# Node chain of a graph layer: its intermediate in a PSUM bank, the bias added by VectorE, and another order of the first loads

## The chip, the cores and the metric

One core of a Trainium2 chip runs the whole kernel in one launch. The metric is the time on the device in microseconds; of several runs the median counts. The engines have names of their own in the profile: PE is TensorE (PEld its weight loads), DVE is VectorE, ACT is ScalarE, POOL is GpSimd, SP is SyncE, which here only starts transfers.

## What is computed

Two layers with residuals, on x of 6250 rows by 512 and a graph of 106250 edges sorted by target:

```python
x = x + gnn(layernorm(x))       # h = x @ W_self + b_self + mean_over_edges(x[src]) @ W_neigh
                                # layernorm(h) * gamma + beta; h < 0 times alpha; plus x
x = x + ffn(layernorm(x))       # 16 experts, top 2 by a gate; h = silu(x @ w1.T) is averaged
                                # over the tokens of an expert, y = mean @ w2.T,
                                # out = sum over the two picks of softmax weight * y[expert]
```

Everything is float32. The kernel gets that from pairs of float16 numbers, a high and a low part, and three matmuls in place of one (high x high, high x low, low x high).

## The kernel before

A tile is 128 rows of x; there are 49 (TILES), the last with 106 rows. The engines run programs of their own, and semaphores alone order them; each program is written out in the order of work.

**Table (0 to 204 us).** For each tile: SP loads x into one of 8 buffers; VectorE takes the statistics (`stats_of`, L1225) and aggregates; `scales_of` turns four tiles' variances into scale and offset, for the first two groups of four on VectorE (L1236 to L1246), from the third on POOL (L579 to L599). ScalarE applies them (`normal`, L665), TensorE transposes (`turn_x`, L907), ScalarE takes the high part (L673), VectorE the low (`turned_low`, L1251), TensorE multiplies by W_neigh in 12 matmuls (`project`, L861), ScalarE and VectorE take both parts of the result (L681, L1257), and SP stores it to a table in DRAM. Before the first projection VectorE finds the largest weight of W_neigh (L1290), a power of two is derived from it, ScalarE writes the high part of the weights in one instruction (L684) and VectorE the low in one (L1300). ScalarE's queue starts the loads of all weights (L652, L657); SP's queue starts the edge lists (L381 to L389) and then x. Between tiles VectorE has other lists (`lists`): the edge bookkeeping behind tiles 1 to 15, and `self_maxima`, `self_bias`, `self_low` behind tiles 17, 23 and 25. In `self_bias` six instructions write b_self as a high row and a low row of `bparts`.

**Steps (204 to about 1310 us).** 106250 edges are 208 groups of 512; a group can span tiles, so there are 257 steps. POOL fetches 128 rows of 2 KB of the table per indirect gather, four gathers per group (L617), into a ring of four groups; in front of a group it waits for the step that freed the slot. In `step` TensorE adds the rows into the bank of the target tile with one-hot matrices (L960) and counts (L963). Banks 0 and 1 alternate by tile. In the first 45 steps TensorE also computes a `side` per step: bias by one matmul of `kilo` and `bparts` (L934), then x @ W_self in 12 matmuls, in banks 5 and 6, which ScalarE brings to `slots`.

**Node chain.** When a tile's edges are all in, VectorE runs `gnn` (L1324 on): count, sum times share plus self term into `slots` (L1344), memset of the banks (which frees them for the tile after next, `c_ev`), moments, gamma and beta (L1356, L1357), the slope (L1358, L1359), the residual with x loaded anew (L1362), moments, and high and low part of the normalized row (L1367 to L1369). The intermediates `hb`, `ub`, `x2f` lie in SBUF. In tiles 0 to 15 it also takes the maximum of an expert's w1 (L1372), in tiles 20 to 35 it splits w1 in two parts (L1379, L1382), which SP stores and later loads back.

**Tail of the steps.** In the last 49 steps TensorE turns finished tiles (`turn_x2`, L976, through bank 4) and computes gate logits (`gate`); ScalarE copies the turned tile (`take_turned`, L729). VectorE routes the first 32 tiles (`route(0)`) between tiles 46 and 47 and reads their positions, which `place(0)` leaves in bank 5, in `rows_to(0)` between tiles 47 and 48. Then come `route(1)`, the maps, and the first expert gather (L633).

**Experts and output (1373 to 1685 us).** 48 slots of tokens through the experts on TensorE, then the output.

## Time and profile before

| | |
|---|---|
| median of 3 runs | 1687.58 us (1685.50 to 1687.65) |
| profiled execution | 1686.77 us |
| its span, first to last instruction | 1685.0 us |
| busy: PE, DVE, ACT, POOL | 1217.9, 1028.5, 886.9, 992.6 us |
| mean granted TensorE clock | 0.887 of full speed |
| DMA, mean over the span | 228 GB/s |

The profile is of one execution. The busy times are sums over stages with different limits, so none of them is near the span; what matters in a stage is which wait ends last there. Times of matmuls are modelled, and their pitch (start to start) is more telling than their length.

### The profile page before, as it was taken

The numbers are of one execution on the slowest core, as the hardware profiler recorded it, in microseconds if no ns is written. First come the engines' busy times: TensorE is split into PE (matmuls) and PEld (weight loads), VectorE is DVE, ScalarE is ACT, GpSimd is POOL, SyncE is SP. The second block draws the span as 40 slices with busy tenths as digits, with TensorE's granted clock in tenths as the row PEclk, the third lists the DMA queues.
The fourth block names the chain that finished last, engine by engine and source line by source line (L and its number), as shares of the span: only waits on it lengthen the run. The fifth ranks groups of instructions, "written<-read, shape, count | busy, mean of one in ns | idle before, by whom it ended". The sixth has DMA issues, their size and how long they took to land.

```text
span 1685.0 us, 37100 instructions
## 1 busy us (share of the span) xinstructions
PE 1217.9 (72%) x7688; PEld 644.5 (38%) x7696; DVE 1028.5 (61%) x2918; ACT 886.9 (53%) x1932; POOL 992.6 (59%) x1193
## 2 busy tenths in 40 slices
PE   4989899999665555665565546666677159999876
PEld 2545444444322222222222222234444146777612
DVE  6676235546666665657566655655658966666626
ACT  3455445555644444444444444446667838888402
POOL 2223277676777777777777777777776025555200
PEclk9999999999988888778878897799999669999885
DMA  5445277777888887888888888778877526666547
GB/s 194 141 139 166 108 219 252 243 250 225 265 265 268 264 245 237 280 260 296 261 281 279 285 279 275 240 237 249 246 233 219 216 80 201 199 200 205 192 167 275
DMA packets 141638, 384.99 MB, mean 228 GB/s; under 512 B 22911, under 2 KB 23041, under 8 KB 141509
## 3 DMA queue, kind: packets, MB, share of 16 engines
q0 software_dynamic: 75840, 248.18, 48.9%
q1 hardware_dynamic: 62392, 130.43, 21.8%
q10 hardware_dynamic: 3276, 4.97, 0.9%
q8 instruction: 43, 0.70, 0.2%
q14 instruction: 87, 0.70, 0.1%
HBM read 323.78 MB, written 59.72 MB: 228 GB/s over the span
## 4 chain that ended last, share of the span: by engine, by line
PE 39%; POOL 24%; issue 16%; DVE 9%; DMA 7%; POOLq 2%; SPq 2%; ACT 1%; DVEq 0%; ACTq 0%
POOL work L617 24%; PE ps L861 13%; PE ps L960 10%; PE ps L1053 6%; DMA work<-table,work 4%; PE ps L1064 3%; PE ps L1055 3%; POOLq L612 2%; PE ps L1113 1%; SPq L525 1%; DMA work<-in_w_t 1%; DMA work<-in_x 1%; PE ps L907 1%; DVE slots L1515 1%; PE ps L934 1%
## 5 line engine op out<-in xcount | busy, mean ns | idle before, releaser
L617 POOL DMA_INDIRECT work<-table,work x832 | 828.4, 996 | 295.6 <-issue 239.8
L960 PE MATMUL ps<-work 128*128 x2056 | 574.6, 431 | 345.0 <-DMA work<-table,work 329.5
L960 PEld LDWEIGHTS ps<-work 128*128 128x128 f16 x2056 | 216.4, 106 | 589.9 <-issue 445.3
L715 ACT ACTIVATE work<-work,ones 128x512 f16<-128x512 f16 x259 | 185.3, 715 | 325.7 <-PE ps L963 325.2
L709 ACT ACTIVATE work<-iota_row,work 128x128 f16<-128x128 f32 x1040 | 331.3, 390 | 31.6 <-ACT work L715 23.9
L861 PE MATMUL ps<-wparts,slots 128*128 128x512 f16 x1176 | 274.1, 383 | 12.2 <-DVE slots L1251 12.2
L1339 DVE TENSOR_SCALAR inv<-ps 128x1 f32 (+2 forms) x49 | 7.7, 158 | 336.6 <-PE ps L963 331.9
L633 POOL DMA_INDIRECT slots<-x_d,betab x114 | 107.8, 946 | 161.8 <-PE ps L1064 83.9
L861 PEld LDWEIGHTS ps<-wparts,slots 128*128 128x128 f16 x1176 | 115.8, 99 | 139.8 <-DVE slots L1251 14.7
L1053 PE MATMUL ps<-work,wparts 128*128 x456 | 156.1, 382 | 2.2 <-ACT wparts L801 2.0
L801 ACT COPY wparts<-ps 128x1024 f16<-128x1024 f16 x114 | 115.3, 1012 | 59.8 <-PE ps L1064 59.1
L1055 PE MATMUL ps<-work,wparts 128*128 x456 | 125.0, 274 | 0.0
L1553 DVE TENSOR_REDUCE work<-ps 128x256 f32<-128x512 f32 x114 | 78.7, 691 | 41.4 <-PE ps L1055 40.3
L963 PEld LDWEIGHTS ps<-onesh,work 128*128 128x128 f16 x1028 | 68.3, 102 | 76.5 <-issue 28.5
L729 ACT COPY wparts<-ps 128x1024 f16<-128x1024 f16 (+1 forms) x49 | 49.4, 1009 | 81.3 <-PE ps L976 80.2
L721 ACT ACTIVATE slots<-ps,wscale 128x512 f32<-128x512 f32 (+1 forms) x49 | 33.6, 686 | 103.0 <-PE ps L861 103.0
L1545 DVE TENSOR_TENSOR slots<-slots,work 128x256 f32 x114 | 52.8, 464 | 39.2 <-issue 24.5
L1064 PE MATMUL ps<-identh,slots 128*128 128x128 f16 x912 | 70.8, 221 | 5.1 <-DMA slots<-x_d,betab 5.1
L1064 PEld LDWEIGHTS ps<-identh,slots 128*128 128x128 f16 x912 | 61.4, 99 | 20.3 <-issue 5.3
L681 ACT ACTIVATE work<-ps 128x512 f16<-128x512 f32 (+1 forms) x49 | 29.2, 596 | 75.7 <-PE ps L861 75.7
L587 POOL TENSOR_SCALAR var<-mv 128x4 f32<-128x4 f32 x11 | 2.5, 228 | 108.3 <-DVE mv L1233 108.3
L963 PE MATMUL ps<-onesh,work 128*128 128x1 f16 x1028 | 64.1, 166 | 0.0
(283 smaller groups left out, 1577.5 us busy)
## 6 DMA issues: line engine op xcount, KB each, us to landing
work<-in_x SPq DMA_DIRECT2D x96, 256.0 KB, 2.8
work<-in_w_t SPq DMA_DIRECT2D x48, 512.0 KB, 7.6
work<-table,work POOLq DMA_INDIRECT x832
table<-work SPq DMA_DIRECT2D x48, 256.0 KB, 2.0
x_d<-work SPq DMA_DIRECT2D x48, 256.0 KB
x_d<-slots SPq DMA_DIRECT2D x48, 256.0 KB
out_x<-slots SPq DMA_DIRECT2D x48, 256.0 KB
slots<-x_d SPq DMA_DIRECT2D x41, 256.0 KB
```

Source lines behind the costliest of these rows:

```text
L617: pool.indirect_dma_start(out=gath[:, g % GRING, w, :], out_offset=None, in_=table[:, :], in_offset=bass.IndirectOffsetOnAxis(ap=idx_all[: ...
L633: pool.indirect_dma_start(out=xf[:, b, :], out_offset=None, in_=x2_d[:, :], in_offset=bass.IndirectOffsetOnAxis(ap=idx2[:, k:k + 1], axis= ...
L709: last = act.activation(away[:, par, w, :], iota_row[:, :], ACT.Abs, bias=negd[:, ds(GT * k + w, 1)])
L715: act.activation(hot[:, slot, :, :], away[:, slot % 2, :, :], ACT.Relu, bias=ones[:, 0:1], scale=-1.0).then_inc(c_hot, 1)
L801: act.copy(xft[:, b, :, :, :], chunks16(bank16(6 + n % 2), P)).then_inc(f_xt, 1)
L861: last = pe.matmul(to, left(a, c), right(w, c), start=start and c == 0 and a == 0 and w == 0, stop=c == n - 1 and a == 1)
L960: pe.matmul(ps[:, ds(bank, 1), :], hot[:, s, w, :], gath_row[:, ds(at + (2 * w + half) * D, D)].unsqueeze(1), start=False, stop=True, skip ...
L963: last = pe.matmul(ps[:, BANKS:2 * BANKS, 0:1][:, ds(bank, 1), 0], hot[:, s, w, :], onesh[:, :], start=False, stop=True, skip_group_check= ...
L1053: pe.matmul(ps[:, HBANK + b, :].rearrange("p (u a n) -> p u a n", u=1, a=2), xft[:, b, 0, c, :], both, start=c == 0, stop=c == CHUNKS - 1, ...
L1055: last = pe.matmul(ps[:, HBANK + b, FF:2 * FF].unsqueeze(1), xft[:, b, 1, c, :], high, start=False, stop=c == CHUNKS - 1, skip_group_check ...
L1064: last = pe.transpose(bank16(6 + n % 2)[:, j * P:(j + 1) * P], xf[:, b, j * P:(j + 1) * P], identh[:, :])
L1553: dve.tensor_reduce(hid[:, b, :], ps[:, HBANK + b, :].rearrange("p (a n) -> p n a", a=2), X, ALU.add).then_inc(f_pre, 1)
```

## The change

- `gnn`: PSUM bank 4 (`draft`) is the intermediate. L1344 writes there, a tensor_tensor adds `bself` on VectorE, and each instruction that had `hb`, `ub` or `x2f` beside another SBUF tensor has one input from the bank. `hb` stays in SBUF for one of them. `ub` and `x2f` are gone.
- `side`: the bias matmul is gone, and so are `kilo`, `bparts` and their preparation. `bself` stays in SBUF until the last tile, so expert 14's part of w1, which lies over it, is among the last four loaded.
- w1 split: the low part is written in two halves, each by a tensor_scalar into the bank and a tensor_tensor from it.
- `turn_x2` goes through bank 5, with new waits in front of it and of `place(0)`.
- Start: SP loads x 0 to 3 ahead of the edges; the other weights are loaded from POOL's queue behind its `scales_of(0)`; all scales are now POOL's; the W_neigh parts are written in four chunks each, behind `normal(0)` and `normal(1)`, and TensorE waits for them chunk by chunk.

```diff
@@ block.sync
+            for i in range(HALF):
+                load_x(i)
             early = (GROUP_CHUNKS - 1) * P * GE_EDGES
...
-            for i in range(UNROLL):
+            for i in range(HALF, UNROLL):
                 load_x(i)
...
-            for e in list(range(9)) + list(range(12, EXPERTS)):
+            for e in list(range(9)) + [12, 13, 15]:
                 load_w1s(e)
...
-            for e in range(9, 12):
+            for e in (9, 10, 11, 14):
                 load_w1s(e)
@@ block.gpsimd
-            for q in range(2, PARTS):
+            scales_of(0)
+
+            for to, what in ((ws[:, :, :], w_self.rearrange("(c p) n -> p c n", p=P)),
+                             (gw[:, :, :], gate_t.rearrange("(c p) n -> p c n", p=P)),
+                             (bself[:, :], b_self.to_broadcast([P, D])), (alphab[:, :], alpha.to_broadcast([P, 1])),
+                             (gammab[:, :], gamma.to_broadcast([P, D])), (betab[:, :], beta.to_broadcast([P, D]))):
+                pool.dma_start(to, what).then_inc(s_w, 16)
+
+            pool.wait_ge(s_const, 2)
+            for n, s in enumerate(c_g):
+                pool.dma_start(spare[16 * n:16 * (n + 1), :],
+                               zero[16 * n:16 * (n + 1), :].bitcast(f16)).then_inc(s, 16 * GT)
+            pool.dma_start(x2_d[0:1, :], zero[0:1, :].bitcast(f16)).then_inc(d_zero, 16)
+
+            for q in range(1, PARTS):
                 scales_of(q)
@@ block.scalar
-            act.wait_ge(w_scale, 1)
-            act.activation(wnp[:, 0, :, :], wn[:, :, :], ACT.Copy, scale=wscale[:, 0:1]).then_inc(w_hi, 1)
             normal(0)
             normal(1)
+            act.wait_ge(w_scale, 1)
+            for c in range(CHUNKS):
+                act.activation(wnp[:, 0, c, :], wn[:, c, :], ACT.Copy, scale=wscale[:, 0:1]).then_inc(w_hi, 1)
@@ block.tensor
-                pe.matmul(to, kilo[:, 0:rows], bparts[:, :], start=True, stop=False)
-                split_mm(to, lambda a, c: xt[:, i, a, c, 0:rows], lambda w, c: wsp[:, w, c, :], CHUNKS,
-                         start=False).then_inc(c_mm, 1)
+                split_mm(to, lambda a, c: xt[:, i, a, c, 0:rows], lambda w, c: wsp[:, w, c, :], CHUNKS).then_inc(c_mm, 1)
...
-                if i:
-                    pe.wait_ge(d_xt, i)
+                pe.wait_ge(d_xt, i) if i else pe.wait_ge(c_self, 2 + TILES)
+                if i == TILES - 2:
+                    pe.wait_ge(i_row, 1)
...
                     if late and k == STEPS - 2:
+                        pe.wait_ge(d_xt, k - LATE)
                         place(0)
@@ block.vector, gnn
+                u, u1 = draft[r, :], draft[r, :].unsqueeze(1)
...
-                ln.link(dve.scalar_tensor_tensor(slot, ps[r, bank, :].unsqueeze(1), share, slot, ALU.mult, ALU.add))
+                ln.link(dve.scalar_tensor_tensor(u1, ps[r, bank, :].unsqueeze(1), share, slot, ALU.mult, ALU.add))
...
+                ln.link(dve.tensor_tensor(u, u, bself[r, :], ALU.add))
...
-                ln.link(dve.scalar_tensor_tensor(hb[r, :].unsqueeze(1), slot, mean, gammab[r, :].unsqueeze(1), ALU.subtract, ALU.mult))
-                ln.link(dve.scalar_tensor_tensor(hb[r, :], hb[r, :], guess[r, 0:1], betab[r, :], ALU.mult, ALU.add))
-                ln.link(dve.tensor_scalar(ub[r, :], hb[r, :], 0.0, alpha_less[r, :], ALU.min, ALU.mult))
-                ln.link(dve.scalar_tensor_tensor(ub[r, :], ub[r, :], shift1, hb[r, :], ALU.add, ALU.add))
+                ln.link(dve.scalar_tensor_tensor(u, u, mean, gammab[r, :], ALU.subtract, ALU.mult))
+                ln.link(dve.scalar_tensor_tensor(hb[r, :], u, guess[r, 0:1], betab[r, :], ALU.mult, ALU.add))
+                ln.link(dve.tensor_scalar(u, hb[r, :], 0.0, alpha_less[r, :], ALU.min, ALU.mult))
+                ln.link(dve.scalar_tensor_tensor(u, u, shift1, hb[r, :], ALU.add, ALU.add))
...
-                dve.scalar_tensor_tensor(x1, x1, up1, ub[r, :], ALU.mult, ALU.add).then_inc(d_x1, 1)
+                dve.scalar_tensor_tensor(x1, x1, up1, u, ALU.mult, ALU.add).then_inc(d_x1, 1)
...
-                dve.tensor_scalar(x2f[r, :], x1, mean, unit, ALU.subtract, ALU.mult)
+                dve.tensor_scalar(u, x1, mean, unit, ALU.subtract, ALU.mult)
                 ln.link(dve.tensor_scalar(hi, x1.unsqueeze(1), mean, unit, ALU.subtract, ALU.mult))
-                dve.tensor_tensor(lo, x2f[r, :].unsqueeze(1), hi, ALU.subtract).then_inc(d_x2, 1)
+                dve.tensor_tensor(lo, u1, hi, ALU.subtract).then_inc(d_x2, 1)
...
-                    dve.scalar_tensor_tensor(halved[:, :, 1, :], stage[:, :, :], wscale[:, 3:4], halved[:, :, 0, :],
-                                             ALU.mult, ALU.subtract).then_inc(v_split, 1)
+                    for h in range(2):
+                        cs = slice(h * CHUNKS // 2, (h + 1) * CHUNKS // 2)
+                        u2 = draft.rearrange("p (c n) -> p c n", c=CHUNKS // 2)
+                        dve.tensor_scalar(u2, stage[:, cs, :], wscale[:, 3:4], None, ALU.mult).then_inc(v_hi, 1)
+                        dve.wait_ge(v_hi, 4 * (j - SPLIT_AT) + 2 + 2 * h)
+                        dve.nop(nofuse=True)
+                        lo2 = dve.tensor_tensor(halved[:, cs, 1, :], u2, halved[:, cs, 0, :], ALU.subtract)
...
```

## Rows read from the trace of the kernel before

**Rows 1.** The page, the chain that ended last, by line.
```profile
POOL work L617 24%; PE ps L861 13%; PE ps L960 10%; PE ps L1053 6%; DMA work<-table,work 4%; PE ps L1064 3%; PE ps L1055 3%; POOLq L612 2%; PE ps L1113 1%; SPq L525 1%; DMA work<-in_w_t 1%; DMA work<-in_x 1%; PE ps L907 1%; DVE slots L1515 1%; PE ps L934 1%
```

**Rows 2.** The gathers' line L617: durations, then what POOL sat idle for (us, times).
```profile
L617 POOL DMA_INDIRECT work<-table,work x832: 940/946/1771, 204.0 to 1299.1; - x167
  issue: 239.8, 787
  PE ps L963: 28.1, 44
```

**Rows 3.** Chain of waits, 1255 to 1385 us: start, us, what.
```profile
1266.87 0.76 DVE slots L1344
...
1372.87 0.94 POOL slots L633
```

**Rows 4.** Groups by line, POOL, 424 to 1263 us: busy, mean ns | idle.
```profile
L617 POOL DMA_INDIRECT work<-table,work x644 | 643.8, 1000 | 196.2 <-issue 186.8 <-PE ps L963 9.4
```

**Rows 5.** Timeline, a split tile, 716 to 720 us: start, us, engine, line.
```profile
716.48 0.55 DVE L1367 TENSOR_SCALAR work<-work,norm 128x512 f32<-128x512 f32 x1
716.54 1.06 POOL L617 DMA_INDIRECT work<-table,work  x1 [0.30 <-issue]
...
719.10 1.28 DVE L1382 SCALAR_TENSOR_TENSOR work<-work,wscale 128x1024 f16<-128x1024 f32 x1
...
719.44 1.76 POOL L617 DMA_INDIRECT work<-table,work  x1 [0.30 <-issue]
```

**Rows 6.** Windows: us; busy PE, PEld, DVE, ACT, POOL; clock, DMA share, GB/s.
```profile
686.00:1032.00 346.00, 198.49 (x961) 91.44 (x962) 225.03 (x698) 158.97 (x400) 266.73 (x261) 0.83 0.86 278
```

**Rows 7.** Chain of waits, 217 to 227 us, a pattern of 45 pitches.
```profile
217.57 0.24 PE ps L934
217.80 2.59 PE ps L861 x12
...
222.20 0.24 PE ps L934
```

**Rows 8.** Groups by line and form, DVE, 686 to 1032 us.
```profile
L1382 DVE SCALAR_TENSOR_TENSOR work<-work,wscale 128x1024 f16<-128x1024 f32 x15 | 19.3, 1284 | 1.8
...
L1369 DVE TENSOR_TENSOR slots<-work,slots 128x512 f32 x15 | 10.4, 692 | 2.2
...
L1367 DVE TENSOR_SCALAR work<-work,norm 128x512 f32<-128x512 f32 x15 | 8.3, 554 | 0.6
...
L1358 DVE TENSOR_SCALAR work<-work,alpha_less 128x512 f32<-128x512 f32 x16 | 7.8, 487 | 0.6
L1346 DVE MEMSET ps<- 128x512 f32 x15 | 7.3, 485 | 0.9
...
L1339 DVE TENSOR_SCALAR inv<-ps 128x1 f32 x15 | 2.4, 157 | 82.0 <-PE ps L963 78.2 <-issue 3.9
```

**Rows 9.** Timeline of the start.
```profile
7.82 2.29 DVE L1290 TENSOR_REDUCE wmax<-work 128x1 f32<-128x2048 f32 x1 [7.68 <-DMA work<-in_w_neigh]
...
16.82 0.38 DVE L1238 BATCH_NORM_AGGREGATE mv<-stats 128x2 f32<-128x6 f32 x4
...
19.96 0.16 DVE L1246 TENSOR_SCALAR gb<-nmr 128x4 f32<-128x4 f32 x1
...
23.54 3.33 PE L861 MATMUL ps<-wparts,slots 128*128 128x512 f16 x12
...
34.24 4.45 PE L861 MATMUL ps<-wparts,slots 128*128 128x512 f16 x12 [3.90 <-DVE slots L1251]
```

**Rows 10.** Timeline of POOL, 36 to 45 us: first and last of a scale chain.
```profile
38.34 0.25 POOL L587 TENSOR_SCALAR var<-mv 128x4 f32<-128x4 f32 x1 [27.97 <-DVE mv L1233]
...
43.38 0.22 POOL L599 TENSOR_SCALAR gb<-nmr 128x4 f32<-128x4 f32 x1
```

**Rows 11.** Chain of waits, 84 to 130 us, around the bias list.
```profile
104.28 2.78 PE ps L861 x12
...
111.73 2.76 PE ps L861 x12
```

More of the change, by code:

```diff
@@ L236, in build @@
         wall = cut(P)
-        assert place[0] <= WORK - TABLES
+        assert place[0] <= BSELF_AT
         BT = BATCH[0][1]
@@ L554, in _ @@
             pool.memset(onesh[:, :], 1.0)
-            pool.memset(kilo[:, :], SCALE)
             pool.memset(zero[:, :], 0.0)
@@ L1288, in _ @@
             dve.wait_ge(s_const, 1)
+            for i in part_tiles(0):
+                last = stats_of(i)
+            ln.link(last)
+            dve.nop(nofuse=True)
+            scales_of(0)
             dve.wait_ge(s_wn, 16)
```

110 lines of the change are left out of this document (43 added, 67 removed).

## The prediction

> **What bounds the kernel now.** I read the page's chain first: one line, L617, the indirect gathers of the step stage, carries 24% of the span as POOL work [rows 1]. The line's own view says how such a gather goes: typically 946 ns, at worst 1771, and in front of 787 of 832 of them POOL waits for nothing that shows, 239.8 us in all, 0.305 each [rows 2]. So a bare gather costs 0.946 + 0.305 = 1.251 us. The same view puts TensorE in front of 44 gathers, 28.1 us; less the 0.305 that every gap has, 28.1 - 44 x 0.305 = 14.7 us are real waits, for steps that free a ring slot. After 424 us no gap is longer than the usual one, so all 14.7 lie before it.
>
> From that I see four stretches. From 0 to 204 us the table is built: TensorE, now and then held up by VectorE. From 204 to about 424 TensorE is the bound, which there has the self terms beside the steps. From 424 to 1264 it is POOL, gather behind gather. From 1267 it is VectorE: tile 46, the first routing batch, tiles 47 and 48, routing and maps, to the first expert gather at 1372.87 [rows 3]. Behind that the change touches nothing that is late.
>
> The gathers of the third stretch aren't bare: 644 of them take 643.8 us where 644 x 0.946 = 609.2 would do, 34.6 too much [rows 4]; in the 346 us with the w1 split 261 take 266.7 in place of 246.9, 19.8 too much [rows 6]. The timeline shows who lengthens them [rows 5]: the gather that starts 0.34 us into the 1.28 us scalar_tensor_tensor of the w1 split (L1382, two SBUF inputs) takes 1.76 us and ends 0.82 behind that instruction's end. One that starts with a tensor_scalar (L1367, one SBUF input) takes 1.06.
>
> **The change, part by part.**
>
> *The intermediate in PSUM.* The large instructions of a node chain with two SBUF inputs are L1356, L1357, L1359, L1362, L1369, and L1382 in 16 tiles. Each of them gets one input from bank 4 instead, or (L1382) gives way to tensor_scalars into the bank and tensor_tensors out of it. If two SBUF inputs are what holds a gather, the 34.6 us go, but for what L1368 and L1379 do, which keep one SBUF input and an SBUF output. A hit costs 1.06 - 0.95 = 0.11 us by the row [rows 5]; one hit in each of some 40 tiles would be 4.4, I take a third, 1.6 (bounds 0 and 8, the latter in the first rival): -33.0 us. POOL waits for nothing else here, so this is the span's, as long as the transfers follow: the DMA engines are busy 0.86 [rows 6], and the same bytes in 4% less time are 0.90.
>
> The Trainium skill (SBUF — State Buffer, Who interferes with whom) says that a VectorE instruction with two SBUF inputs contends with a GpSimd instruction that reads SBUF and that the later one is blocked; the gather of 1.76 us agrees. It also says that a tensor_scalar in a two-port mode blocks GpSimd for its whole length; the gather of 1.06 us, which started with the 0.55 us L1367, doesn't bear that out fully. By that rule L1368 and L1379 would go on holding gathers.
>
> *The bias matmul.* In the second stretch each pitch of 4.63 us has a piece of 0.24 us of L934 on the chain [rows 7]. A matmul of 512 columns has a pitch of 2.59/12 = 0.216 there [rows 7], and 48 of the 49 lie in the stretch: -10.4 us. POOL's real waits are 14.7, which is more, so it doesn't become the bound. If some of it does, -6.
>
> *VectorE's extra work.* Per tile there is one tensor_tensor 128x512 more, 0.69 and a gap of 0.04. L1358 and L1367 have 0.49 and 0.55 us for 512 elements, where the two-input forms and L1382 (1.28 for 1024) go at half the rate; into PSUM I give them 0.75. That is +0.27 and, since L1368 starts 0.47 behind the start of L1367, +0.27. Together 1.27 us per tile [rows 8]. The one large VectorE output in PSUM that the trace has is the 0.485 us memset, so an output there costs between nothing extra and, by doubling 0.75, 0.75 more. I take nothing, as the row is near.
>
> In the middle this hides. VectorE waits 82.0 us for TensorE in front of L1339 in the 15 tiles of the split's 346 us [rows 8], 5.5 each; the tile pitch is 832/49 = 17 gathers of 266.7/261 + 0.305 = 1.33, 22.6 us. So it is occupied 17.1. To that come 1.27 and, for the split, two times 0.75, two times 0.69 and gaps of 0.3 in place of 1.28 and 0.1: +1.8. That makes 20.2 against a new pitch of 17 x 1.251 = 21.3: just hidden. In the last stretch nothing hides it: three tiles, +3.8 us.
>
> The Trainium skill (VectorE: DVE Perf Modes, The TRN2 errata) gives a PSUM source 120 fixed cycles and an SBUF source 58, 0.065 us more; by that the tail would be some 8 instructions x 3 tiles x 0.065 = 1.6 us longer. No row here shows that difference.
>
> *Turn bank and waits.* The transposes move to bank 5, where the first batch's positions come too. place(0) now waits for a ScalarE copy, with the last step behind it; VectorE comes to the positions 2.5 us later than before and to the last tile 3.8 later, so both should hide. turn_x2(47) waits until VectorE has read the positions; behind it are two gates, and on ScalarE a copy, a distance and the one-hots that SP's w1 loads wait for. The next to need any of them is tile 48's transpose, a whole node chain later. Nothing, or +3 if it doesn't hide. Four w1 loads instead of three come last; I take nothing, for the first expert gather comes some 36 us after they are issued.
>
> *Start.* Before, the first scale chain on VectorE goes from the aggregates at 16.82 to the last scale at 20.12, project(0) starts at 23.54 and project(2), behind the second such chain and the edge list, at 34.24 [rows 9]. After, x 0 to 3 come together with the neighbour weights (2 MB by about 8.5 us, an estimate from 1.5 MB by 7.8); statistics and aggregates to 9.4, POOL's scale chain of 5.3 us [rows 10] to 14.7, two normals of 0.8 to 16.2, four chunks of the high part of 0.6 to 18.6, the low part to 19.9, project(0) near 20.7: 2.9 earlier. VectorE also is rid of 2.9 of the second chain's 3.3 us: 5.8 at best by project(2), of which I take 4.5, since TensorE and ScalarE are late next. Against it: POOL issues six weight loads and five small stores ahead of scales_of(1). No row has a 512-row load in its queue. At 0.5 us each (a small one) they are hidden; at four times a gather's 0.95 for the two large ones, normal(4) comes late by 2 us. Bounds -1 and -6.
>
> *Self lists.* VectorE's bias list stops TensorE once: 7.45 us between two projections whose pitch is 3.03 each, so 1.4 are lost [rows 11]; they go, and the reduction of b_self, an instruction of 0.69, too: -2.1.
>
> **Sum:** -33.0 - 10.4 + 3.8 - 4.5 - 2.1 = -46.2 us. The span 1685.0 becomes 1638.8, and with the 1.77 that lies around it in the profiled execution (1686.77) 1640.6. The median of the runs, 1687.58, is 0.8 above that execution: 1641.4 us.
>
> **The rivals.**
> *Tensor_scalars hold gathers as well.* L1368 (0.55) and L1379 (0.75) then cover a gather's start with the chance length/1.25 and hold it for half their length: 0.12 us in each of 39 tiles and 0.22 in each of 16, 8.2 us where I have 1.6: 1648. For it speaks that L1368 would be the largest of its kind left; against it the 1.06 us. Chance 0.13.
> *The rate isn't POOL's to give.* The transfers, at 0.86 busy, can't come faster, or the two inputs aren't what lengthens a gather: only -13.2 is left, 1674. For it: 278 GB/s in the split tiles [rows 6]. Against: no wait for a slot after 424. Chance 0.10.
> *VectorE becomes the bound in the 16 split tiles.* The price is paid per output into PSUM. The two banks let it lag by one tile, 21 us, so it decides from 21.3 + 21/16 = 22.6 us a tile, and from 25.4 it eats the whole gain. At 0.75 more for each of 8 large outputs a tile takes 26.2: 16 x 4.9 - 21 = +57, and in the tail 3 x 6 x 0.75 = +13.5: 1712. Against it is the memset. Chance 0.04.
> The forecast has 0.70, with a range of its own of 1634 to 1650; 0.03 is for what I don't see.
>
> **Range and chances.** 1631 to 1661: the low end has start and self lists at their best and no residue; the high end takes the first rival, a poor start, the dearer tail and a part of the second rival. This kernel's measurement tells 0.2%, 3.4 us, from no change. The first two rivals are faster as well: faster 0.94, same 0.02, slower 0.04.
>
> **What would show it.** L617 in the third stretch at a mean of 0.95 us, none near 1.7, about 790 in all. L934 gone and the pitch 4.42 in the second. First gather at 197.4, project(0) near 20.7. L1358 and L1367 at 0.75, the wait in front of L1339 in the split tiles about 1 us each. 110 us in place of 106 from tile 46's eviction to the first expert gather. Wrong would be: gathers beside instructions with one SBUF input above 1.1 us, gathers that wait for TensorE after 415 us, large outputs in PSUM above 0.9 us, or project(2) no earlier than 33.

## The result, and the profile after

The changed kernel takes 1643.49 us (median of 4 runs, 1643.22 to 1646.05) where the kernel before takes 1686.54 (4 runs, 1684.44 to 1687.65). The ratio is 0.9746, with a 95% interval of 0.9731 to 0.9760. The profiled execution has 1643.22 us and a span of 1641.4, 43.6 less than the 1685.0 of before. Forecast were 1641.4 us.

The page's chain by line has the old order: the gathers, now line L626, still lead it, with 22% in place of 24% [rows 1], and the bias matmul's line is gone from it.
```profile
POOL work L626 22%; PE ps L866 14%; PE ps L967 11%; PE ps L1062 6%; DMA work<-table,work 5%; PE ps L1073 3%; PE ps L1064 3%; POOLq L621 2%; PE ps L1122 1%; DMA work<-in_w_t 1%; SPq L526 1%; DMA work<-in_x 1%; PE ps L912 1%; DVE slots L1520 1%; DVE slots L1486 1%
```

The gathers' own line (durations, then what POOL sat idle for, us and times). The longest gather is 1347 ns where it was 1771, the median is the same 946 [rows 2]: what a gather costs by itself has not changed, and most of the lengthened ones have gone. Of 95 gathers over 1.1 us 7 are left; the 1347 ns stand beside a two-input instruction of the routing (L1445), which the change didn't touch. The real waits for TensorE are 26.1 - 54 x 0.305 = 9.6 us; they were 14.7.
```profile
L626 POOL DMA_INDIRECT work<-table,work x832: 940/946/1347, 197.8 to 1249.8; - x167
...
  issue: 236.7, 777
...
  PE ps L970: 26.1, 54
```

Groups by line, POOL, in the stretch that it bounds, 413 to 1216 us (answers to [rows 4]): the mean is 948 ns where it was 1000. 607.9 - 641 x 0.946 = 1.5 us of excess are left of 34.6.
```profile
L626 POOL DMA_INDIRECT work<-table,work x641 | 607.9, 948 | 195.7 <-issue 184.0 <-PE ps L970 11.6
```

Windows of the same stretch and of the 326 us with the w1 split (us; busy PE, PEld, DVE, ACT, POOL; clock, DMA share, GB/s; answers to [rows 6]): the same work in less time fills the DMA engines to 0.89, at 293 GB/s, where it was 0.86 and 278. They followed.
```profile
413.00:1216.00 803.00, 487.74 (x3083) 246.65 (x3080) 590.96 (x1761) 419.34 (x1019) 607.61 (x641) 0.88 0.86 272
659.00:985.00 326.00, 190.25 (x970) 89.68 (x968) 261.67 (x736) 159.15 (x401) 246.92 (x260) 0.87 0.89 293
```

VectorE by line and form in those 326 us (answers to [rows 8]). L1379 and L1382 are the new split, L1361 and L1352 the two tensor_scalars that now write PSUM, L1362 and L1373 those that still write SBUF, L1339 the bias add. The last row is the wait for the next tile: 21.3 us for 16 of them, where it was 82.0 for 15.
```profile
L1379 DVE TENSOR_SCALAR ps<-work,wscale 128x512 f32<-128x512 f32 x30 | 22.6, 754 | 3.2
L1382 DVE TENSOR_TENSOR work<-ps,work 128x512 f16<-128x512 f32 x30 | 20.8, 692 | 3.1
...
L1361 DVE TENSOR_SCALAR ps<-work,norm 128x512 f32<-128x512 f32 x15 | 12.2, 814 | 0.6
L1336 DVE SCALAR_TENSOR_TENSOR ps<-ps,inv,slots 128x512 f32<-128x512 f32 x15 | 11.4, 759 | 3.7 <-DVE inv L1334 3.7
...
L1373 DVE TENSOR_SCALAR work<-work,wscale 128x1024 f16<-128x1024 f32 x15 | 11.3, 755 | 0.0
L1352 DVE TENSOR_SCALAR ps<-work,alpha_less 128x512 f32<-128x512 f32 x15 | 11.3, 754 | 0.5
...
L1339 DVE TENSOR_TENSOR ps<-ps,work 128x512 f32<-128x512 f32 x15 | 9.5, 636 | 0.0
L1362 DVE TENSOR_SCALAR slots<-work,norm 128x512 f32 x15 | 8.7, 581 | 0.0
...
L1331 DVE TENSOR_SCALAR inv<-ps 128x1 f32 x16 | 2.5, 158 | 21.3 <-issue 14.7 <-PE ps L970 6.7
```

The second stretch, chain of waits: a pitch is 215.24 - 210.82 = 4.42 us. The 0.24 us piece of [rows 7] is gone.
```profile
210.82 2.61 PE ps L866 x12
213.43 1.73 PE ps L967 x8
215.16 0.08 PE ps L970 x4
215.24 2.61 PE ps L866 x12
```

The end of the third stretch and of the fourth, chain of waits. Tile 46's eviction is at 1219.56 and the first expert gather at 1329.49 (1266.87 and 1372.87 in [rows 3]).
```profile
1213.78 3.10 DMA work<-table,work
...
1219.56 0.77 DVE ps L1336
...
1329.49 0.94 POOL slots L642
```

With these readings the 43.6 us of the span fall into five parts (us; start times of gathers number 0 and 160, of tile 46's eviction and of the first expert gather, and the rest):

| stretch | before | after | difference | forecast |
|---|---|---|---|---|
| start of the kernel to gather 0 | 204.0 | 197.8 | -6.2 | -6.6 |
| gather 0 to gather 160 | 220.0 | 209.9 | -10.1 | -10.4 |
| to tile 46's eviction | 842.8 | 811.9 | -31.0 | -33.0 |
| to the first expert gather | 106.0 | 109.9 | +3.9 | +3.8 |
| rest | 312.1 | 311.9 | -0.2 | 0 |

The first row isn't all the change's. In the profiled execution of before, TensorE's granted clock is 0.5 of full speed (1.2 GHz) for 3.4 us from 35.0 us on, after TensorE had been idle for 3.90 us [rows 9]; project(2) takes 4.45 us there. In that of after no such stretch comes in the table stage, TensorE had been idle for 1.78 us, and project(2) takes 2.76. So 1.7 of the 6.2 us are the clock's (windows of before and of after, columns as above).
```profile
35.00:38.40 3.40, 3.40 (x10) 1.06 (x7) 3.14 (x9) 0.00 (x0) 0.06 (x1) 0.50 0.38 132
31.20:33.90 2.70, 2.70 (x13) 1.10 (x13) 2.70 (x5) 2.20 (x4) 0.00 (x0) 1.00 0.04 14
```
It is no fixed cost of the old start: no_bias_mm below, which starts like the kernel before, takes 2.76 us there after 3.21 us of idle time, and node_only, which has the old start as well, takes 4.28 at a clock of 0.5.

### The profile page after: what moved, and what is told of

Read it like the earlier page. It is cut to its first block, busy times and chain, and to the rows that moved or that the text cites. A ratio compares the mean times of both kernels' runs of the same rounds, so it can differ in the third digit from the quotient of the medians.

```text
span 1641.4 us, 37307 instructions
## 1 busy us (share of the span) xinstructions
PE 1189.9 (72%) x7639; PEld 636.6 (39%) x7647; DVE 1109.4 (68%) x2978; ACT 887.4 (54%) x1935; POOL 966.4 (59%) x1236
## 4 chain that ended last, share of the span: by engine, by line
PE 40%; POOL 22%; issue 16%; DVE 9%; DMA 7%; POOLq 2%; SPq 1%; ACT 1%; DVEq 0%; ACTq 0%
POOL work L626 22%; PE ps L866 14%; PE ps L967 11%; PE ps L1062 6%; DMA work<-table,work 5%; PE ps L1073 3%; PE ps L1064 3%; POOLq L621 2%; PE ps L1122 1%; DMA work<-in_w_t 1%; SPq L526 1%; DMA work<-in_x 1%; PE ps L912 1%; DVE slots L1520 1%; DVE slots L1486 1%
## 5 line engine op out<-in xcount | busy, mean ns | idle before, releaser
L626 POOL DMA_INDIRECT work<-table,work x832 | 790.0, 950 | 290.6 <-issue 236.7
L967 PE MATMUL ps<-work 128*128 x2056 | 557.4, 421 | 330.6 <-DMA work<-table,work 316.4
L866 PEld LDWEIGHTS ps<-wparts,slots 128*128 128x128 f16 x1176 | 112.1, 99 | 140.0 <-DVE slots L1249 13.8
L726 ACT ACTIVATE slots<-ps,wscale 128x512 f32<-128x512 f32 (+1 forms) x49 | 33.6, 686 | 92.7 <-PE ps L866 92.7
L1255 DVE SCALAR_TENSOR_TENSOR work<-ps,work 128x512 f16<-128x512 f32 (+1 forms) x49 | 33.7, 689 | 44.1 <-ACT work L685 44.0
## 6 DMA issues: line engine op xcount, KB each, us to landing
work<-in_w_t SPq DMA_DIRECT2D x48, 512.0 KB, 12.2
```

Of the source, the lines that this page charges most:

```text
L626: pool.indirect_dma_start(out=gath[:, g % GRING, w, :], out_offset=None, in_=table[:, :], in_offset=bass.IndirectOffsetOnAxis(ap=idx_all[: ...
L866: last = pe.matmul(to, left(a, c), right(w, c), start=start and c == 0 and a == 0 and w == 0, stop=c == n - 1 and a == 1)
L967: pe.matmul(ps[:, ds(bank, 1), :], hot[:, s, w, :], gath_row[:, ds(at + (2 * w + half) * D, D)].unsqueeze(1), start=False, stop=True, skip ...
```

## Experiments: does each part bring its share alone?

All ratios are to the kernel before on the same chip, with 95% intervals. The gathers' total is the sum of the durations of the 832 gathers. Each trace is of one execution; those of no_bias_mm, node_only, dummy_ts, bias_sbuf and best are the longest of their kernel's.

**start_only.** The kernel before with the new start alone: the two loads' order, POOL's scale chains, the chunks of the neighbour weights.

> The kernel before with the new start alone (x 0 to 3 first, other weights from POOL's queue, all scales on POOL, neighbour weights in chunks); node chain, bias matmul and bias list as before. Theory: the start is worth what the table stage shows of it, 4.75 us at project(3), and the rest of the 6.2 us at the first gather comes from the shorter lists: first gather at 199.3, time 1681.8 (-4.8). Rival: the start's gain is eaten again in the table stage by VectorE's lists, so that the first gather comes less than 2 us earlier. In the gathers nothing changes: L617's total stays near 828 us.

Measured: 1687.4 us, ratio 0.9979 (0.9966 to 0.9992), -3.5 us. The first gather starts at 200.4 where it was 204.0, -3.6 and not the -4.7 expected. Project(3) starts at 35.30 where it was 40.26, 5.0 earlier, 1.7 of them by the clock as above; but then the granted clock is 0.5 for 3.4 us from 100.0 on, the projection there takes 4.45 us instead of 2.76, and 1.7 are lost again. The last gather starts at 1299.4, where it was 1299.1: the gathers' total is 833.1 us in place of 828.4, with the same longest one. So in this execution the gathers took back what the start gave, and the median shows less than was expected. What is held varies by some 4 us with nothing changed: 790.0 and 794.5 in two executions of the changed kernel (the second is after_again below).

**no_bias_mm.** The kernel before without the bias matmul; it leaves b_self out of the result.
```diff
-                pe.matmul(to, kilo[:, 0:rows], bparts[:, :], start=True, stop=False)
-                split_mm(to, ..., CHUNKS, start=False).then_inc(c_mm, 1)
+                split_mm(to, ..., CHUNKS).then_inc(c_mm, 1)
```

> The kernel before without the bias matmul (b_self is left out of the result); VectorE's preparation of it stays. Theory: TensorE is the bound while it has sides, so 48 x 0.216 = 10.4 us go, time 1676.2, and POOL's real waits for steps fall from 14.7 to about 4. Rival: POOL is as late as TensorE there, and the gathers, still lengthened, give only 6 us or less. 260 to 420 us is the only stretch that gets shorter; L617's total stays near 828.

Measured: 1680.2 us, ratio 0.9944 (0.9927 to 0.9960), -9.4 us. The gathers, source view (columns as above):
```profile
L617 POOL DMA_INDIRECT work<-table,work x832: 940/946/1770, 202.2 to 1292.9; - x167
...
  issue: 236.4, 776
...
  PE ps L961: 23.2, 55
```
The real waits are 23.2 - 55 x 0.305 = 6.4 us, 8.3 less than before. From gather 0 to gather 160 it is 210.2 us where it was 220.0, -9.8: in its stretch the matmul's 10.4 us are worth nearly all of it. The rest of this trace doesn't stand still, and its span is only 5.4 shorter: the first gather comes 1.8 earlier (the clock at project(2)), the third stretch takes 2.8 more with a total of 832.4 in place of 828.4, and from tile 46's eviction to the first expert gather it is 110.1 us in place of 106.0, since VectorE waits 4.15 us for TensorE's positions, which the kernel before reaches without a wait. So the last stretch isn't VectorE's alone; TensorE's last steps are close behind.

**node_only.** The kernel before with the node chain and the w1 split through bank 4 and nothing else: old start, bias matmul kept, no bias add.

> The kernel before with one part of the change: the node chain's intermediate and the low part of the expert weights go through a PSUM bank. The old start, the bias matmul and the bias rows of the self list stay, and VectorE adds no bias. Theory (the parts add up): the gathers' total falls from 828 to about 795 us with none near 1.7 us, pitch 4.63 stays in the second stretch, first gather near 204, and with no bias add the stretch from tile 46's eviction to the first expert gather stays at 106: time before less 33, ratio 0.980. Rival (how much the gathers gain hangs on when the chain happens to run, which the bias matmul and start shift): 0.985 or more, with several two-port instructions of the chain holding gathers to 1.4 us or longer.

Measured: 1655.49 us, ratio 0.9810 (0.9793 to 0.9827), -32. The gathers' total is 793.5 us where it was 828.4. From tile 46's eviction (1238.51) to the first expert gather (1346.20) it is 107.7 us: 1.7 more than before without a bias add, and the bias add makes the 109.9 of the change.
```profile
L620 POOL DMA_INDIRECT work<-table,work x832: 943/949/1337, 203.5 to 1268.1; - x167
```
The 107.7 are not the 106 expected; they agree with the forecast's 0.27 + 0.27 us for each of three tiles. So the parts add up: by the ratios, of 1687 us each, the three runs give -32.1, -9.4 and -3.5, with +2.2 for the bias add -42.8; the whole change gives -43.1 by its medians. Each of the three has an interval of 2 to 3 us to either side, so the sum shows that nothing large is missing, and no more.

## Experiments: what lengthens a gather?

A gather is called held here when it ends 0.80 to 0.83 us behind the end of a VectorE instruction and takes over 0.99 us. The traces also show that nothing but lengthened gathers costs time in the third stretch. From the start of gather 160 to that of gather 780 there are 620 pitches, 620 x 1.251 = 775.6 us; what a trace has more is the excess of these gathers over 0.946 us, to within 0.7 us, in every trace but dummy_ahead's: 809.2 us with an excess of 33.8 before, 777.2 with 1.4 after, 820.1 with 44.6 in chain_sbuf, 797.1 with 21.7 in bias_sbuf. From gather 780 to tile 46's eviction it varies more, from 30.6 to 35.7 us, and by 3.1 between two executions of the changed kernel (34.6 and 31.5); why isn't known.

**chain_sbuf.** The changed kernel with the intermediate in SBUF; the w1 split stays in halves and goes through that SBUF buffer too. The buffer takes room, so in this run and in the three with a useless instruction expert 13's part of w1 is also among the last loaded; behind the first expert gather these kernels take 310.9 to 312.9 us, where the changed one has 311.9.
```diff
-        hb = cut(D)
+        hb, draft = cut(D), cut(D)
-        draft = ps[:, DRAFT_AT, :]
```

> The changed kernel with one thing undone: the intermediate lies in SBUF (a buffer of the same size) and not in bank 4; bias add, split in halves, start and turn bank stay. Theory (two SBUF inputs hold a gather): the gathers' total rises from 790 by 30 to 38 us, those that start under a two-input instruction end 0.82 us behind its end, time about 1673 (+30, with 1.5 less in the tail from faster tensor_scalars). Rival (bank 4 isn't what matters, the gathers were lengthened by something else that the change took away): total stays within 5 us of 790 and the time within 3 us of 1643.5.

Measured: 1689.91 us, ratio 1.0001 (0.9985 to 1.0016). The whole gain is lost and more than the forecast 30 us: the gathers' total is 847.4, more than before the change. The longest gather is 1928 ns:
```profile
L625 POOL DMA_INDIRECT work<-table,work x832: 941/946/1928, 198.5 to 1298.8; - x167
```
The mechanism is confirmed, the size isn't explained: this kernel has one large two-input instruction per tile more than the kernel before, the bias add, and by my price of 0.18 us for one it should cost 9 us; 37 of 48 of them hold a gather, for 18.0 us.

**split_old.** The changed kernel with the old scalar_tensor_tensor for the low part of w1, all else in PSUM.

> The changed kernel with the old w1 split (one tensor_scalar and one scalar_tensor_tensor of 1024 elements with two SBUF inputs) in its 16 tiles; the node chain stays in bank 4. Theory: the one long instruction costs what the 16 split tiles had beyond the others before, 19.8 - 16 x 0.6 = 10 us: L626's total 800, gathers of up to 1.76 us, time 1653.5; the 1.8 us per tile that VectorE saves are worth nothing. Rival (VectorE nearly fills the split tiles, and its load costs time): the relief is worth something and the time rises by less than 5 us.

Measured: 1649.7 us, ratio 0.9767 (0.9749 to 0.9784), +3.5 us against the changed kernel by the ratios and +5.7 by the spans, where +10 were expected. By the time alone the rival isn't excluded. By the trace it is, for the third stretch: gathers 160 to 780 take 785.9 us, 775.6 and their excess of 10.5, and VectorE's relief takes nothing off that; 3.2 us less from gather 780 to tile 46's eviction are within what an unchanged kernel varies. All 16 of the split's instructions hold a gather, the gathers' total is 799.2, as expected:
```profile
699.03 1.29 DVE L1376 SCALAR_TENSOR_TENSOR work<-work,wscale 128x1024 f16<-128x1024 f32 x1
...
699.33 1.80 POOL L626 DMA_INDIRECT work<-table,work  x1 [0.30 <-issue]
```
The gather ends at 701.13 and the instruction at 700.32: 0.81 us between, as in [rows 5].

**after_again, dummy_tt, dummy_ts.** The first is the changed kernel once more, to have it on the same chip as the others. The other two add a useless instruction right behind the memset of the accumulator bank in 28 of the 49 tiles (0 to 19 and 36 to 43), where VectorE has time for it: a tensor_tensor with two SBUF inputs (0.67 us) or a tensor_scalar with one (0.68 us).
```diff
                 dve.memset(ps[:, bank, :], 0.0).then_inc(c_ev, 1)
+                if extra:
+                    dve.tensor_tensor(scrap[:, :], bself[:, :], gammab[:, :], ALU.add)
# or
+                    dve.tensor_scalar(scrap[:, :], negd[:, 0:2 * D], 1.0, None, ALU.mult)
```

> The changed kernel itself, for a time on the same chip as the runs beside it and for a second trace. Expected: 0.9746 of the kernel before within 0.2%, and the gathers' total at 790 us again, within 3.

> The changed kernel with one useless instruction more in 28 tiles (0 to 19 and 36 to 43, none in the split tiles), right behind the memset that frees the bank: a tensor_tensor 128x512 with both inputs and the output in SBUF, about 0.69 us. It stands where the bias add stood in the run with the intermediate in SBUF; there 35 of 49 such instructions held a gather, 16 us in all. Theory of the place (VectorE's chain starts a fixed time behind a landing, so a given instruction meets the gathers always at the same point): 0.33 per tile, the gathers' total rises by 9 us, the time by 6 (part of it lies under TensorE before 410 us). Theory of chance (an instruction covers a gather's start with its length over 1.25): 0.69 x 0.69 / 2 / 1.25 = 0.19 per tile, 5 us in the total, 3.5 in the time.

> As the run beside it, but the useless instruction is a tensor_scalar of 1024 float32 elements from SBUF to SBUF, one tensor input, 0.75 us: at the same place and no shorter. If tensor_scalars of that kind hold gathers for their whole length as the first rival has it, the gathers' total rises by 9 us or more, as with the two-input form. If they cost the 0.11 us of the row in the trace before, it rises by 28 x 0.7 x 0.1 = 2 us and the time by less than 2.

Measured: after_again 1641.93 us, ratio 0.9710 (0.9663 to 0.9757); dummy_tt 1651.65, 0.9764 (0.9714 to 0.9813); dummy_ts 1650.0, 0.9756 (0.9709 to 0.9803). All executions of both lie 5.4 to 11.6 us above those of after_again, though the ratios' intervals meet, as the kernel before varied by 14.5 us on this chip. The gathers' totals are 794.5, 805.6 and 807.2. So one input is as dear as two here, about 0.4 us for each instruction, and my 0.11 us for a hit of a tensor_scalar is wrong as a price. The timeline of dummy_ts at one of them:
```profile
230.38 0.48 DVE L1338 MEMSET ps<- 128x512 f32 x1
230.47 1.81 POOL L626 DMA_INDIRECT work<-table,work  x1 [0.30 <-issue]
...
230.78 0.68 DVE L1340 TENSOR_SCALAR work<-work 128x1024 f32<-128x1024 f32 x1
```
and of the changed kernel at the same place, where a tensor_tensor with one input in PSUM follows the memset:
```profile
230.47 0.48 DVE L1338 MEMSET ps<- 128x512 f32 x1
230.49 0.95 POOL L626 DMA_INDIRECT work<-table,work  x1 [0.31 <-issue]
...
230.86 0.64 DVE L1339 TENSOR_TENSOR ps<-ps,work 128x512 f32<-128x512 f32 x1
```
The held gather ends at 232.28, 0.82 behind the instruction's end, though that instruction started 0.31 us after it.

**bias_sbuf.** The changed kernel with the bias add alone reading two SBUF tiles.
```diff
-                ln.link(dve.scalar_tensor_tensor(u1, ps[r, bank, :]..., share, slot, ALU.mult, ALU.add))
+                ln.link(dve.scalar_tensor_tensor(slot, ps[r, bank, :]..., share, slot, ALU.mult, ALU.add))
-                ln.link(dve.tensor_tensor(u, u, bself[r, :], ALU.add))
+                ln.link(dve.tensor_tensor(u1, slot, bself[r, :].unsqueeze(1), ALU.add))
```

> The changed kernel with one thing undone: the eviction writes its sum to the tile's slot in SBUF and the bias add reads it and b_self there (two SBUF inputs) and writes PSUM; all else of the chain stays in PSUM. The intermediate in SBUF everywhere cost 43 to 46 us where 30 were expected. Theory (place: the bias add stands at a fixed time behind the landing that ends a tile, and so at a fixed time in the gathers' rhythm, and is met nearly each time): the gathers' total goes from 794 to about 810, 30 or more of the 49 bias adds hold a gather to 1.3 us or more, time +14 to +18, near 1658. Rival (chance: 0.18 us for each two-input instruction, as the 196 of the kernel before give, less for the shorter one): 49 x 0.13 = 6 us, total near 800, time near 1649.

Measured: 1656.83 us, ratio 0.9812 (0.9795 to 0.9830), the gathers' total 815.4 (in an execution of 1664.79 us, 8 above the median). The number is the theory's: 38 of 48 bias adds hold a gather, for 22.3 us, 0.46 each. That settles the excess of chain_sbuf. But the theory's reason, a fixed place in the gathers' rhythm, isn't needed. I went through the hits of all these traces one by one and took the start of the VectorE instruction less that of the gather:

| instruction behind | instructions | holds to its end + 0.82 | us in all | latest start behind the gather's that holds |
|---|---|---|---|---|
| memset: dummy_tt | 28 | 20 | 12.5 | +0.44 |
| memset: dummy_ts | 28 | 27 | 13.5 | +0.39 |
| memset: bias add in bias_sbuf | 48 | 38 | 22.3 | +0.47 |
| other: L1357, kernel before | 48 | 21 | 5.8 | -0.1 |
| other: L1356, L1359, L1362, L1369, kernel before | 189 | 68 | 17.3 | -0.1 |
| other: L1382, kernel before, 1.28 us | 16 | 16 | 12.9 | -0.3 |

An instruction behind another that reads holds a gather only if it starts some 0.1 us before it: of the lines in the table's fourth and fifth row 95 started from 0.1 us before to 0.44 us after a gather, and none held it. One behind a memset also holds gathers that started up to 0.4 us before it: 13 of 13 such in dummy_tt and in dummy_ts, 24 of 24 in bias_sbuf, the latest at 0.47; all that started over 0.5 us behind a gather held none. With starts spread evenly over the 1.25 us of a gather's pitch, 0.7 us long, the first kind would hit less than half of the time and the second some four times in five (an estimate from these bounds), and then for longer. A tensor_scalar may also delay the end of a gather that it didn't hold: where it still runs 0.83 us into the gather, the gather ends 0.11 to 0.16 behind it (in the kernel before L1368 13 times, for 1.5 us in all, and L1379 12 times, for 1.9).

**dummy_ahead.** The tensor_tensor of dummy_tt ahead of the two memsets, behind the eviction.
```diff
                 ln.link(dve.scalar_tensor_tensor(u1, ps[r, bank, :].unsqueeze(1), share, slot, ALU.mult, ALU.add))
+                if extra:
+                    dve.tensor_tensor(scrap[:, :], bself[:, :], gammab[:, :], ALU.add)
                 dve.memset(ps[:, BANKS + bank, 0:1], 0.0)
                 dve.memset(ps[:, bank, :], 0.0).then_inc(c_ev, 1)
-                if extra:
-                    dve.tensor_tensor(scrap[:, :], bself[:, :], gammab[:, :], ALU.add)
```

> The same useless tensor_tensor of two SBUF inputs in the same 28 tiles as before, but ahead of the two memsets, right behind the eviction, instead of right behind the memset of the accumulator bank. Of 28 such instructions behind the memset 20 held a gather, for 12.5 us in all (0.45 each), also where the gather had started up to 0.45 us before the instruction. In the kernel before, instructions with two SBUF inputs behind another input-reading instruction held a gather only where they had started at least 0.1 us before it, 0.06 to 0.14 us each (L1356, L1357, L1359, L1362, L1369). Theory (the memset reads nothing, so the instruction behind it takes the shared port about one memset early): here it holds 8 to 12 gathers, 2 to 4 us in all, and no gather that started before it did; gathers' total 795 to 798, time 1643 to 1646 (ratio about 0.974). Rival (what counts is the length and the place in the tile's rhythm behind a landing, 0.7 us earlier here): as many hits as before, total 803 or more, time 1650 or more (ratio 0.9765).

Measured: 2013.89 us, ratio 1.0193 (1.0129 to 1.0258). This run came to a chip on which the kernel before takes 1978.05 us as well, so its time tells nothing of the other chips' kernels. The page of its profile says how that chip differs: in the same 326 us it moves 205 GB/s where the changed kernel has 293, TensorE's granted clock there is 0.72 in place of 0.87, and POOL is busy 185 us in place of 247, because it waits for slots.
```profile
659.00:985.00 326.00, 176.60 (x716) 70.92 (x717) 180.68 (x530) 119.55 (x300) 184.88 (x194) 0.72 0.68 205
```
What the run can still tell is the single hits, and fewer than planned, since most of the 28 instructions met no gather. Two held one, both begun 0.44 us before the gather, 0.2 us in all. Four began 0.01 to 0.46 us after a gather's start and held none, as here:
```profile
242.32 0.95 POOL L626 DMA_INDIRECT work<-table,work  x1 [0.30 <-issue]
...
242.70 0.69 DVE L1338 TENSOR_TENSOR work<-work,gammab 128x512 f32<-128x512 f32 x1
```
The gathers' total is 793.1. That speaks for the memset, on four cases. Both useless instructions and the bias add also don't wait for their predecessor's semaphore, where this one waits for the eviction's; but neither does the tensor_scalar L1373 wait for one, and of 8 of these that started from 0.04 us before to 0.24 us after a gather in the changed kernel none held it to its own end + 0.82. Why the memset matters (it reads nothing, so the next instruction's reads may begin while it runs) is argued and not shown.

## Experiments: a faster version

**sides_half.** In the second stretch of the changed kernel TensorE still bounds: POOL's real waits are 9.6 us. Here a self product is made in every second step instead of in every step.
```diff
-                    if sides and k + AHEAD < TILES:
-                        side(k + AHEAD)
+                    if sides and k % 2 == 0 and k // 2 + AHEAD < TILES:
+                        side(k // 2 + AHEAD)
```

> The changed kernel with one self term per two steps (over 90 steps) in place of one per step (over 45). Theory: the second stretch is TensorE's because each step carries a side; at half the density a pair of steps takes TensorE 2 x 1.81 + 2.61 = 6.2 us, where POOL needs 8.1 for its gathers, so POOL's real waits for steps (54 gaps, 26.1 us, 26.1 - 54 x 0.305 = 9.6) go to about 0 and the time falls by 9 us, to 0.969 of the kernel before. Rival: something else is as late there (landings, ScalarE's copies, or VectorE's node chain at the start), and less than 3 us go.

Measured: 1630.49 us, ratio 0.9654 (0.9604 to 0.9704), 11.4 less than after_again on its chip; 9 were expected. The waits are 12.2 us in 40 times, just the 0.305 of each:
```profile
L627 POOL DMA_INDIRECT work<-table,work x832: 942/946/1343, 198.0 to 1239.9; - x167
...
  issue: 241.0, 791
...
  PE ps L971: 12.2, 40
```

**best.** The same with three more edits: x tile 0 turned behind the first chunk of the weights, the self weights split over four tiles, b_self added to the last three tiles ahead of time.

> The changed kernel with one self product in every second step, and three more edits. (a) Start: ScalarE and VectorE make the high and low parts of x tile 0 behind the first chunk of the neighbour weights instead of behind all four; project(0), which began at 21.30 us, should begin near 19.3: -2 us. (b) The high and low parts of the self weights one chunk in each of four tiles instead of all in one: ScalarE's 1.84 us stall under the list of tile 21 goes: -1.7 us. (c) b_self is added to the self products of tiles 46 to 48 ahead of tile 46's wait, where VectorE idles: three bias adds of 0.64 us and their links leave the tail: -2.0 to -2.7 us. Theory (each piece lies on the path as the chain shows it): about 1624.5 us where the kernel with only the halved self products had 1630.5; first gather at 193 us, 106 us again from tile 46's eviction to the first expert gather's. Rival (the start's gain is eaten by the scales of tiles 4 to 7, which GpSimd finishes at 30.9 us, and (b) by what VectorE does beside it): first gather at 196 to 197 and only the tail's share left: 1628 us.

Measured: 1628.83 us, ratio 0.9653 (0.9640 to 0.9667), no better than sides_half; the rival's time held, though not for its reason. Each edit did something: project(0) starts at 19.06 where sides_half has 21.48, the first gather at 195.6 where it has 198.0 (-2.4), and tile 46's eviction to the first expert gather takes 108.4 us where it takes 110.1 (-1.7).
```profile
19.06 4.55 PE L873 MATMUL ps<-wparts,slots 128*128 128x512 f16 x12 [0.74 <-DVE slots L1256]
```
In the table stage the edits had brought more: up to project(40) TensorE is 4.1 us ahead of sides_half, 2.2 by the start and 1.9 by the spread weights. Then the granted clock is 0.5 for 3.4 us from 162.7 on, behind 1.97 us without work; sides_half, idle for 2.00 us at the same place, doesn't have that, and 1.7 are gone.
```profile
162.28 4.45 PE L873 MATMUL ps<-wparts,slots 128*128 128x512 f16 x12 [1.97 <-DVE slots L1256]
```
The gathers' total rose from 789.6 to 792.9 and the real waits from 0 to 1.0. Gains of 2 us drown in where the clock falls and in how the gathers happen to be met, as in start_only.

## Why the prediction was right, point by point

The order of the four stretches and their bounds held, and the time came out 2.1 us above the forecast.

*The intermediate in PSUM* (-33.0 forecast): the gathers gave 33.1 us of their excess, and 31.0 arrived in the span. The rest went between gather 780 and tile 46's eviction, 34.6 us where it was 33.6; the transfer on the chain there shows 3.10 us, and 1.33 before. The residue was forecast at 1.6 and is 1.5 us, but this is right by luck, and it hides that a term was priced wrongly: I priced a hit at 0.11 us times one tile in three. Measured, a tensor_scalar with SBUF on both sides holds a gather to its end + 0.82 like a two-input instruction, if it starts first; it did so already in the kernel before (L1358 21 times, L1367 11 times). In the profiled execution L1362 does it 6 times in 47 and L1373 8 times in 16, and just for 0.8 and 0.9 us, since they end soon after the gather's start:
```profile
765.54 0.76 DVE L1373 TENSOR_SCALAR work<-work,wscale 128x1024 f16<-128x1024 f32 x1
...
766.09 1.02 POOL L626 DMA_INDIRECT work<-table,work  x1 [0.31 <-issue]
```
In after_again they cost 3.6, in bias_sbuf 5.1. These gathers take up to 1.19 us, so one of the signs of being wrong that I had named, gathers above 1.1 us beside instructions with one SBUF input, did show. The gather of 1.06 us under L1367 [rows 5] wasn't a hit at all: L1367 started 0.06 us before it, too late to hold it, and the 0.11 us are L1368's, which ran until 0.1 before the gather's end. L1361, the same instruction with its output in PSUM, holds none of 47, though it ran across the start of 21 gathers. So the mechanism of the first rival is real, and only its size (8.2 us) is not.

The Trainium skill (SBUF — State Buffer, Who interferes with whom) says that a VectorE instruction with two SBUF inputs contends with a GpSimd instruction that reads SBUF, that one in a two-port mode contends with GpSimd too, for its whole length, and that one with at most one SBUF input outside such modes does not. The runs here agree for both forms, 0.4 us each in dummy_tt and dummy_ts. The same section lets the order of issue decide who waits; but for the 0.1 us this agrees with the instructions that follow a reading one, and not with those behind a memset, which hold gathers that started before them.

*The bias matmul* (-10.4): -10.1 in the change and -9.4 alone. The pitch is 4.42 as forecast, and the real waits, 14.7, were larger than the gain.

*VectorE's extra work* (+3.8): +3.9. Of it 1.7 us come without the bias add (node_only), 2.2 with it; the changed kernel's other traces have 109.9 to 110.2, so this part is steady. Outputs in PSUM cost nothing more for scalar_tensor_tensors (0.759, where L1351, which writes SBUF, has 0.751); the tensor_scalar L1361, whose two scalars are both read from SBUF, took 0.814 for my 0.75, the bias add 0.636 for my 0.69. In the split tiles the forecast was a wait of about 1 us each in front of the eviction, and it is 21.3/16 = 1.3. The third rival (outputs in PSUM dearer) is refuted by these rows.

The Trainium skill (VectorE: DVE Perf Modes, The TRN2 errata) has 120 fixed cycles for a PSUM source and 58 for an SBUF source, which I had made 0.065 us, an estimate. The two scalar_tensor_tensors that write SBUF, now L1351 and L1356 with one input from PSUM, have 0.751 and 0.747; with two SBUF inputs before, as L1357 and L1362, they had 0.753 and 0.752. The difference is not to be seen.

*Start* (-4.5) and *self lists* (-2.1): -6.2 together, for forecast -6.6, and this too is luck. The terms are off one by one, and 1.7 of the 6.2 are the clock's, which the forecast doesn't have: without them the start gave 3.0 for its 4.5. The start of the after kernel (timelines of TensorE, VectorE, POOL and ScalarE):
```profile
9.97 0.38 DVE L1242 BATCH_NORM_AGGREGATE mv<-stats 128x2 f32<-128x6 f32 x4
```
```profile
10.44 0.26 POOL L581 TENSOR_SCALAR var<-mv 128x4 f32<-128x4 f32 x1 [3.25 <-DVE mv L1242]
...
15.76 1.01 POOL L602 DMA_DIRECT2D work<-in_w_self  x1
```
```profile
21.30 4.64 PE L866 MATMUL ps<-wparts,slots 128*128 128x512 f16 x12 [2.73 <-DVE slots L1249]
...
31.18 2.76 PE L866 MATMUL ps<-wparts,slots 128*128 128x512 f16 x12 [1.78 <-DVE slots L1249]
```
```profile
30.92 0.81 ACT L669 ACTIVATE work<-work,gb,gs 128x512 f32<-128x512 f32 x1 [3.87 <-POOL gb L594]
```
Project(0) is at 21.30 for my 20.7, and project(2) at 31.18 where it was 34.24 [rows 9]: 3.1 earlier for my 4.5, and then project(3) 4.7 earlier, the 1.7 more by the clock. The weight loads on POOL cost it 1.01 and 0.79 us for the large ones and 0.56 for the small ones, between my bounds of 0.5 and 3.8; normal(4) did wait for POOL's second chain, 3.87 us, but that wait isn't on the chain: project(2) waits for VectorE, which has the edge list.

The self lists gave 0.7 us and not 1.4 for the stall [rows 11]. The bias list is gone, and behind it ScalarE's high part of the self weights was next (chain of waits):
```profile
98.78 2.76 PE ps L866 x12
...
102.08 0.05 ACT wparts L702
102.13 1.84 issue
...
105.56 2.76 PE ps L866 x12
```
From projection to projection it is 6.78 us where it was 7.45. I had taken the longest of two works under one tile and not looked at the second; best, which spreads it, has 3.03 a projection there.

*The second rival*, transfers that can't come faster: on the chips of all runs but dummy_ahead refuted: 293 GB/s in the split tiles of the changed kernel, and between gathers 160 and 780 no trace has more than 0.7 us of waits beyond the usual gaps. On dummy_ahead's chip, at 205 GB/s, these waits are 294 us; that shorter gathers gain nothing there is argued and not measured. That chip ran neither the changed kernel itself nor a profile of the kernel before, so what the change does there, and why dummy_ahead is 2% slower than the kernel before on it, stays open.

## What to carry to other kernels

When a chain of indirect gathers on GpSimd sets the rate, look at the longest of them and at what VectorE runs when they start: every instruction with two SBUF inputs, and every tensor_scalar from SBUF to SBUF, may hold one until 0.8 us behind its own end, and one operand (or the output) in a PSUM bank ends that. For the two-input forms it cost no VectorE time here, for a tensor_scalar 0.26 us of 0.49 (0.75 in place of 0.49 for 512 columns). Price it as hits times overlap by the instruction's own kind and predecessor, not by one hit from a timeline. Where one work under a tile is taken away, price the second longest at once, for it is what remains. And look at the granted clock before a difference of 2 us between two traces is put down to an edit.

## What the runs showed of the hardware that I had not expected

- A held gather always ends 0.80 to 0.83 us behind the end of the VectorE instruction, whatever that instruction's length (0.49 to 1.29 us) and whichever started first; alone it takes 0.946.
- The instruction behind a memset into PSUM holds gathers that started up to 0.4 us before it, 0.47 at most; 0.45 us for each such instruction in dummy_tt, 0.48 in dummy_ts, against 0.06 to 0.14 for the 0.7 us instructions elsewhere in the kernel before.
- A tensor_scalar from SBUF to PSUM holds none (L1361, 0 of 47; L1379, 0 of 32), one from SBUF to SBUF of the same length does.
- The kernel before took 1687 to 1691 us on four sets of runs and 1978 on the chip of dummy_ahead. In the split tiles dummy_ahead has 205 GB/s and a granted clock of 0.72, the changed kernel elsewhere 293 and 0.87.
- In the table stage the granted clock of TensorE fell to 0.5 for 3.4 us in some traces and at differing places: from 35.0 us in before, 33.6 in node_only, 100.0 in start_only, 162.7 in best, nowhere in after, no_bias_mm or sides_half. In before, start_only and best a projection that otherwise takes 2.76 us took 4.45, and what followed came 1.7 us later.
